# Unread TensorE products in four waits of a two-layer transformer kernel: head of the paged attention, its first block, the wait for the experts' rows, and the wait for the choices

## What is computed

```python
x = x + _L0_attn_ref(_L0_cond_ref(x, ...), ...)
x = x + _L0_ffn_ref(_L0_cond2_ref(x, ...), ...)
x = x + _L1_attn_ref(_L1_cond_ref(x, ...), ...)
x = x + _L1_ffn_ref(_L1_cond2_ref(x, ...), ...)

# _L1_cond2_ref: paged attention, 8 query heads, 4 key heads of 32, window of 128
q = _rope(_rms(q, q_norm_scale), pos); k = _rope(_rms(k, k_norm_scale), pos)
k_blocks = k_blocks.at[blk, :, off, :].set(k.transpose(0, 2, 1, 3))
v_blocks = v_blocks.at[blk, :, off, :].set(v.transpose(0, 2, 1, 3))
k_all = k_blocks[block_tables]...; v_all = v_blocks[block_tables]...
scores = jnp.einsum('bghtd,bgsd->bghts', qg, k_all) * SCALE
p = jax.nn.softmax(jnp.where(allowed, scores, -jnp.inf), axis=-1)
o = jnp.einsum('bghts,bgsd->bghtd', p, v_all)
return jnp.einsum('bto,do->btd', o, Wo)

# _L1_ffn_ref: 16 experts, the best two of each token, and a shared one
topk_val, topk_idx = jax.lax.top_k(jax.nn.softmax(xt @ Wr.T + bias), 2)
y = jnp.einsum('tei,eih->teh', jax.nn.silu(g) * u, Wd)
routed = jnp.einsum('tke,tk,teh->th', oh, w, y)
shared = jax.nn.silu(xt @ sWg) * (xt @ sWu) @ sWd
return routed + shared
```

## Time and profile before

| | us |
|---|---|
| median of 3 runs | 584.53 (583.47 to 586.75) |
| the profiled execution | 580.49 |
| its span, first to last instruction | 578.7 |
| TensorE busy (matmul) | 495.7 (86%) |
| VectorE busy | 359.3 (62%) |
| GpSimd busy | 261.9 (45%) |
| ScalarE busy | 252.8 (44%) |
| TensorE's mean granted clock | 0.931 |

### The profile page before, as it was taken

How to read it: one execution, slowest core, us unless ns; L and a number is a source line. 1 busy time by engine, 2 the same in 40 slices (tenths; PEclk the granted TensorE clock), 3 DMA queues, 4 the chain that set the end, 5 groups by cost and what they waited for, 6 DMA issues and landing times. The chain is left out here.

```text
span 578.7 us, 10881 instructions
## 1 busy us (share of the span) xinstructions
PE 495.7 (86%) x4207; PEld 375.7 (65%) x4207; DVE 359.3 (62%) x777; ACT 252.8 (44%) x548; POOL 261.9 (45%) x240
## 2 busy tenths in 40 slices
PE   2997799999998999998879899477999998199956
PEld 0686368886886788776644347356777775099846
DVE  2757478886686878845676555953466886334412
ACT  6287753343432444243872334363355544034420
POOL 5055435463443677775650000378572017445640
PEclk9799999999999999999999899756699999689987
DMA  5564681000000121230000009511000002498326
GB/s 172 185 253 171 263 242 42 1 1 1 0 1 1 37 71 57 68 102 16 2 3 1 1 1 353 192 40 26 14 26 5 3 1 82 158 332 257 112 71 195
DMA packets 24723, 51.53 MB, mean 89 GB/s; under 512 B 4264, under 2 KB 16705, under 8 KB 23520
## 3 DMA queue, kind: packets, MB, share of 16 engines
q1 hardware_dynamic: 18704, 40.62, 20.4%
q0 software_dynamic: 5968, 10.22, 5.9%
HBM read 43.99 MB, written 12.37 MB: 97 GB/s over the span
## 5 line engine op out<-in xcount | busy, mean ns | idle before, releaser
L753 PE MATMUL ps<-x_split,gate_up_split 128*128 128x512 f32 x384 | 96.3, 393 | 0.1
L753 PEld LDWEIGHTS ps<-x_split,gate_up_split 128*128 128x128 f32 x384 | 72.0, 188 | 17.1 <-issue 1.5
L2055 POOL DMA_INDIRECT wbig<-new_kv,prepi x40 | 42.4, 1059 | 79.8 <-DVE wmid L1443 68.7
L940 POOL TENSOR_TENSOR gate_up_split<-wbig,gate_up_split 128x768 fp32r<-128x768 f32 (+1 forms) x24 | 41.5, 1731 | 52.3 <-ACT gate_up_split L882 52.2
L864 DVE TENSOR_TENSOR hidden_split<-work,hidden_split 128x512 fp32r<-128x512 f32 x34 | 37.7, 1109 | 23.1 <-ACT hidden_split L929 23.1
L775 PE MATMUL ps<-hidden_split,down_split 128*128 128x512 f32 x160 | 42.5, 395 | 2.6 <-issue 1.4
L1995 POOL DMA_INDIRECT chosen<-work,wbig x31 | 30.5, 984 | 30.8 <-ACT work L1980 16.6
L929 ACT ACTIVATE hidden_split<-work 128x512 fp32r<-128x512 f32 x34 | 21.4, 630 | 50.6 <-DVE work L859 48.4
L946 POOL TENSOR_TENSOR down_split<-wbig,down_split 128x384 fp32r<-128x384 f32 (+1 forms) x24 | 29.1, 1213 | 25.9 <-ACT down_split L889 25.8
L2055 POOL DMA_INDIRECT wbig<-in_cache_dram,prepi x32 | 33.5, 1047 | 7.6 <-issue 6.9
L775 PEld LDWEIGHTS ps<-hidden_split,down_split 128*128 128x128 f32 x160 | 29.8, 188 | 10.7 <-issue 4.2
(11 more groups left out here) (337 smaller groups left out, 1180.1 us busy)
## 6 DMA issues: line engine op xcount, KB each, us to landing
work<-in_wE_dram SPq DMA_DIRECT2D x1, 5376.0 KB, 16.1
wbig<-in_wF_dram SPq DMA_DIRECT2D x3, 1664.0 KB, 7.0
sorted<-wmid SPq DMA_DIRECT2D x1, 3999.0 KB, 16.8
wbig<-in_wG_dram SPq DMA_DIRECT2D x1, 3072.0 KB, 10.3
wbig<-in_wE_dram SPq DMA_DIRECT2D x6, 384.0 KB
wbig<-chosen SPq DMA_DIRECT2D x8, 256.0 KB, 5.1
wbig<-sorted SPq DMA_DIRECT2D x1, 1935.0 KB, 12.8
wmid<-in_wE_dram SPq DMA_DIRECT2D x5, 384.0 KB
```

The lines of the kernel that those rows point to most:

```text
L753: mm = nc.tensor.matmul(o, self.gus[:, w % 2, a, 2 * m + k, :], self.xs[:, b, k, n * HALF:(n + 1) * HALF], start=(k == 0 and a == b), stop ...
L940: nc.gpsimd.tensor_tensor(self.gus[:, k % 2, 1, 0:self.gu_chunks], self.gate_up[:, :, j * P:(j + 1) * P], self.gus[:, k % 2, 0, 0:self.gu_ ...
L2055: return nc.gpsimd.indirect_dma_start(dst, None, table, bass.IndirectOffsetOnAxis(ap=rows.bitcast(U32), axis=0), **({} if bound is None el ...
```

## The change

A function `unread(n, bank)` is added. It issues n products of the identity with the first 512 columns of `small`, all in float32, into one bank of `ps`. No instruction reads what they write. They carry no semaphore. They are called at eight places of TensorE's program with 59 products in all: 2 behind the projections and 2 behind the turned output weights, 9 between the two halves of the queries, 8 behind the second half, 2 in the first iteration of the page loop, 14 behind the shared expert, 7 behind the wait for `sent`, and 15 behind the last tile. Four waits come with them: for `page_v_raw` 2, for `sent`, for `tile_h` 31, and the existing wait for `page_raw` now stands behind the first two products. No instruction is removed, and the other engines' programs are as they were.

```diff
+        def unread(n, bank):
+            for _ in range(n):
+                nc.tensor.matmul(ps[:, bank, :], ident, small[:, 0:512], start=True, stop=True)
...
+            pe.wait_ge(sem("page_v_raw"), 2)
+            unread(2, 3)
             pe.wait_ge(sem("page_raw"), 4)
...
             tr.then_inc(sem("fold_turned"), 1)
+            unread(2, 3)
             pe.wait_ge(sem("fold_kept"), 1)
...
                     tr.then_inc(sem("page_qt"), 1)
+                if n == 0:
+                    unread(9, 3)
+            unread(8, 7)
             pe.wait_ge(sem("page_qm"), 16)
...
                     scores(b + 1)
+                if b == 0:
+                    unread(2, 7)
...
             pe.wait_ge(sem("ffn_h_ready"), moe.count("h_ready", 2))
+            unread(14, 5)
             pe.wait_ge(sem("ffn_out"), moe.count("out", 4))
             pe.wait_ge(sem("ld_wE_low"), 16)
+            pe.wait_ge(sem("sent"), 16 * 2 * NT)
+            unread(7, 5)
             for t in range(N_TILE + 2):
...
+            pe.wait_ge(sem("tile_h"), N_TILE)
+            unread(15, 0)
             for g in range(NT):
                 if g % 2 == 0:
                     pe.wait_ge(sem(f"chosen{g // 2}"), 32)
```

## The result

| | before | changed |
|---|---|---|
| median of 6 runs each, same chip, us | 585.03 (583.47 to 586.75) | 589.66 (586.14 to 592.41) |
| the profiled execution | 580.49 | 586.14 |
| its span | 578.7 | 584.4 |
| TensorE's mean granted clock | 0.931 | 0.977 |

The changed kernel takes 1.0079 of the time of the one before, with an interval of 1.0043 to 1.0115: it is slower by 2.5 to 6.7 us, most likely 4.6. The forecast was 583.7, with a range up to 589. The sum was made against the profiled execution: -0.8 us was forecast and +5.65 came. Medians here are of all executions; ratios and their intervals leave out those over 1.5% above their kernel's fastest, so a ratio need not be the quotient of two medians.

What follows compares the result with a forecast made beforehand. TensorE, busy 86% of the span and partly at its lower clock of 1.2 GHz, was taken as the bound. Page -5.8, experts +2.9, combining +2.1 gave -0.8 on 584.53: 583.7 us, range 577 to 589.

Steps and rivals of the forecast that it cites:

- Price of a product: Each unread float32 product on TensorE was to take 0.857 us at full clock, 50.6 us for all 59.
- Rival 3: Each unread product costs only 0.23 us, so nothing overruns: -16 us, 568; chance 0.06.
- Head: Page head: 2, 2, 9 and 8 products delay the first scores from 383.00 to about 386.95, +3.95 us.
- Page loop: Page's scores and values at full clock: scores(11) at 413.3 instead of 419.12, so -5.8 us for the page.
- the copy: Page loop: ScalarE's copy of the second keys had waited 1.95 us; half was taken, 1 us in the sum.
- My nearer bound: Page: with all old stalls whole and the clock kept, the page would still win, -4.8 us.
- Rival 4: Clock falls in the thin stretch around 391 to 393, before the first values: +10.7 us, 595; chance 0.07.
- rival 1: Clock falls back after the first values' stall, the next group taking 4.35 us more: 588.0, slower; chance 0.17.
- Experts: 14 and 7 products start the first tile 4.9 us late; full clock leaves +2.9 us at gate_up(2).
- Combining: 15 products start the combining 4.9 us late; full clock wins 2.8 there, leaving +2.1 us.
- The sum: Page -5.8, experts +2.9 and combining +2.1 give -0.8 us, no change that can be told.
- The base of the sum: The median lay 4.0 us above the profiled execution, place unknown; the difference was put on the median, 584.53.

Runs made afterwards that it cites:

- head_only: The changed kernel with only the page's 23 products (2, 2, 9, 8, 2): 583.25 us, 1.0003 of the kernel before.
- change_again: The changed kernel measured once more, nothing altered: 577.47 us, 1.0142 of the kernel before.
- combine_only: The changed kernel with only the 15 products before the combining: 587.02 us, 1.0066 of the kernel before.
- experts_only: The changed kernel with only the 14 and 7 products before the experts and the wait for the sends: 590.01 us, 1.011 of the kernel before.
- fit_no_head: The changed kernel with 14 products before the experts, 9 before the combining, none elsewhere: 584.08 us, 0.9895 of the kernel before.
- fit: The changed kernel with batches cut to their waits (2, 2, 6, 4, 0; 14 and none; 9): 579.69 us, 0.9918 of the kernel before.
- fit_old_head: The changed kernel with the page's 2, 2, 9, 8, 2 kept, then 14 and none, and 9: 584.74 us, 0.9939 of the kernel before.
- before_look: The kernel before, unchanged, profiled once more: 568.13 us, 1.0028 of the kernel before.
- fit_no_head_again: Repeat of fit_no_head, beside change_again: 565.17 us, 0.9948 of the kernel before.
- fit_again: Repeat of fit, beside change_again: 565.32 us, 0.9971 of the kernel before.
- few_gathers_head_2: The kernel before with 8 of 40 gathers of new rows and the page's 23 products, a repeat: 569.16 us, 1.0055 of the kernel before.
- set 3: Third group of follow-up runs, on one chip: change_again, the change with 9 products before the combining, fit_again, fit_no_head_again; kernel before 568.16 us.
- set 4: Fourth group, on one chip: before_look and repeats with 8 of 40 gathers, the page's 23 products, or both; kernel before 567.20 us.

## Why the prediction was wrong

**Price of a product: right.** 9 in 7.73, 8 in 6.87, 21 in 18.02 and 15 in 12.88 us of the chain that ended last, 0.858 to 0.859 each. The sum took 0.857. Rival 3, with 0.23 us, is out, and with it the 216 ns of the Trainium skill (TensorE: Matmul & The Clock Gate, Back-to-back issue gap) for this type of data: the trace does not agree, by a factor of four.

**Head: right.** Scores(0) at 386.98, forecast 386.95. The second half's transposes at 377.67 with 377.8 forecast, the keys at 385.42 with 385.5.

**Page loop: this is the step that failed.** Forecast was -5.8, with bounds of -11.8 and -4.8; the profile has -2.1 and the medians of head_only nothing. The loop was laid out as "scores(4) starts at 394.1, the first values at about 398.8", with the stall of 3.4 us "whole" at the first values and 1 us for the copy, 17.25 us from scores(0) to scores(7). It came to 20.77 (386.98 to 407.75), which is 3.5 of the 3.7 us that the term missed. change_again is the same kernel in a profile without such a stall and with the clock at 1.00: 7.16 us from scores(0) to scores(4), where 7.15 were forecast, and 14.43 to scores(7), where the sum less its 4.4 us of stalls has 12.85. So 1.6 us of the miss lie in the layout behind scores(4); 1.2 of it is a wait for one VectorE multiplication, which took 1.94 us there and 0.41 to 0.48 around it. The other 1.9 are the stalls and the clock: they cost 6.3 us where the sum had 4.4. Of these 3.1 fell ahead of scores(4), where the maximum of sequence 2 (counted from 0) and the copy stood at full clock, and 3.2 behind it, where the maximum of sequence 3 stood and then the clock was at 0.50. At the first values nothing stood. My nearer bound, "all whole and the clock kept", kept the clock by assumption; that was no bound.

**Where the stalls stand.** The working tied each stall to an instruction. The profiles rather tie them to time. Counted from the end of the projections, with GpSimd's first gather 5.1 to 5.3 us behind it in every profile, the first stall begins at 25.6 or 25.7 us in the four kernels of the front and the first two sets whose head has no products (before, combine_only, experts_only, fit_no_head), and at 25.9 in the changed kernel and head_only; fit and fit_old_head have their first of over 1 us at about 32. In the same way the first values took 3.8 to 5.3 us in the five kernels of those sets that began them 36.7 to 38.1 us behind the projections, and 1.1 in the three with the full head, which began them at 42.1 to 43.9. In two of the five this stretch ends at 42.5 and 42.6, in the others between 40.5 and 43.3. So the 3.4 us weren't won by the clock: the later loop reached the first values when that stretch was all but over, and met the earlier stalls with other instructions. What happens at these times the traces don't show.

**Rival 4 had the place, rival 1 the size.** Rival 4 let the clock fall in the thin stretch at the second keys, ahead of the first values, if the granted clock dropped between 386 and 395. It dropped between 396 and 397, behind that very stretch. Its price was too high, +10.7 against +5.65, because it let the first values stall as before. Rival 1 let the clock fall behind the first values, at 588.0 close to the measured 589.66; there the clock was 1.00 again, so that its size came near is luck. The Trainium skill (TensorE: Matmul & The Clock Gate, Why this matters for your kernels) advises keeping TensorE busy and gaps short; the rows agree as far as they go: the fall followed 2 us with 0.44 of work in the changed kernel, and 2 us with 0.47 in the old trace. What the rows add is that two products put in one iteration ahead of a stall don't carry the clock over it.

**Shared expert: not in the forecast.** It was taken over unchanged, and lost 1.6 us through a clock that fell behind a wait of 2.08 us; the same wait had not done it before. change_again, before_look and fit_no_head_again take 8.7 us for this stage, as the earlier trace rows do; fit_again and few_gathers_head_2 lose the same 1.6 us, and the second has no product behind the page. Between the last scores and the end of these products the clock falls in 13 of the 18 profiles, at 448 to 482 us and in kernels with and without added products. So this is scatter from execution to execution, and no effect of the change that any run shows.

**Experts: right within 0.2 in this execution.** Forecast 4.9 late at the first tile and +2.9 at gate_up(2); from the shared expert's end it was 5.0 late and +3.1. In set 3 the delay is plain: the first tile starts 18.05 us behind the shared expert in change_again and 13.0 in fit_no_head_again, and the tile loop takes 48.5 us in both, so there all 5.0 us are lost. The seven products behind the wait for the sends bought nothing that the 14 hadn't.

**Combining: right within 0.3.** Start 13.4 behind the last product instead of 8.4 (+5.0, forecast 4.9), length 7.31 instead of 9.97 (-2.7, forecast -2.8). What the forecast missed is only seen once the overrun is gone: `chosen` sets the pace of the first two quarters.

**The sum.** With -2.1 for the page, +1.6 for the shared expert, +3.1 and +0.7 for the tiles and +2.4 for the combining the execution is explained. What decided between no change and slower was the page, the term with the widest bounds. The two overruns were costs wherever they were measured: with 0 + 9 in place of 7 + 15, with or without the page's products, the ratios were 0.9895 to 0.9971, four of five clear of 1.

**The base of the sum.** The prediction put the median 4.0 us above its execution and could say nothing on where. In the later profiles of the front's kernel and its variants the projections end at 364.9 to 371.1 us, against 364.7 in the front: up to 6 us of scatter lie ahead of everything that the change touches.

**Best version.** fit_no_head has 14 products before the experts, 9 before the combining, and nothing else: 0.9895 and 0.9948 of the kernel before in two sets, 565.17 against 577.47 us for the change in the same set. Its profile in set 3 shows the work: the products end before the waits do, and the combining follows 8.5 us behind the last product of the tiles.

```profile
480.87 12.18 PE L1448 MATMUL ps<-small 128*128 128x512 f32 x28
...
542.87 7.89 PE L1448 MATMUL ps<-small 128*128 128x512 f32 x18
550.80 2.05 PE L1952 MATMUL ps<-small,wbig 128*128 128x128 f32 x16
553.08 5.62 PE L1952 MATMUL ps<-small,wbig 128*128 128x128 f32 x48 [0.23 <-DMA wbig<-chosen]
```

**Open.** What makes VectorE and ScalarE stand in some sets and not in others; whether the part ahead of the experts that one profile of experts_only shows explains the 3 us above its sum in the median; and why the three places alone add to 10.2 us where the whole was 4.6 in its first measurement.

## What to carry to other kernels

Work put into a wait to hold the clock must end before the wait does: on an engine that runs in order every microsecond of overrun delays all that follows, and the higher clock gave back 2 to 2.7 of 5 us here at best. Price the filler from a row of its own type (float32 products of 512 columns took 0.857 us), fill to a little less than the wait, and leave alone a stage that comes to full clock by itself in its first few groups. A stall without a releaser may be tied to time and not to the instruction that it hits: when the work moves, another instruction meets it. It may also be gone in the next execution. Look at a second profile before a term of a sum rests on it, and at every fall of the clock in the old one.

## What the runs showed of the hardware

- One and the same kernel had medians of 583.05, 589.92, 568.16 and 567.20 us in four sets. Most of the difference lies in the page loop in the two profiles of it: scores(0) to scores(31) took 76.6 us in the front, 61.1 in set 4. In the profiles of the first two sets and of the front, VectorE or ScalarE waited up to 5.7 us in the loop with no releaser, in every kernel with 40 gathers; in the last two sets no kernel shows any.
- The first of those waits began 25.6 to 25.9 us behind the end of the projections in six of the eight profiles that have any of over 1 us, with TensorE's queue as before and with the 23 products in it.
- The clock can fall in one execution and not in another at the same place: behind a wait of 2.08 us the shared expert's first products ran at 0.50 in the changed kernel's profile, and not in that of the kernel before.
- Unread products of the identity with constants hold the granted clock as other products do: 1.00 all through 18 us before the tiles.
